# A fused macaron transformer block: two steps of VectorE's queue change places with the next item's cosines

## The reference, cut to what matters

```python
x = x + 0.5 * L0_ffn(layernorm(x))     # FFN stage, first time
x = x + L0_attn(layernorm(x))          # 16 heads, linear position bias
x = x + 0.5 * L0_ffn(layernorm(x))     # FFN stage, second time
x = x + 0.5 * L1_ffn(layernorm(x))     # mixture of 8 experts, top 1
x = x + L1_attn(layernorm(x))          # linear attention
x = x + 0.5 * L1_ffn(layernorm(x))
```

```python
h = shift_token(x); q, k, v = split(h @ wqkv)           # 8 heads of 64
q = l2norm(q) * qs; k = l2norm(k) * ks
q = q*cos*scale + rotate_half(q)*sin*scale               # k likewise with /scale
attn = softmax(mask(8 * q @ k.T)); x = x + (attn @ v) @ wo
h = layernorm(shift_token(x)) * g + b
a, g = split(h @ w1 + b1); x = x + (a * gelu(g)) @ w2 + b2
```

## Time and profile before

| | value |
|---|---|
| median of 3 runs | 2471.24 us (2462.63 to 2471.93) |
| profiled execution, own time | 2476.3 us |
| its span, first to last instruction | 2474.5 us |
| PE busy | 2133.3 us (86%) |
| DVE busy | 1762.1 us (71%) |
| ACT busy | 1464.2 us (59%) |
| POOL busy | 1056.6 us (43%) |

### The profile page before, as it was taken

One profiled execution on the slowest core, in us unless ns is written; L12 is line 12 of the kernel. 1 busy time (PEld: TensorE's weight loads), 2 busy tenths in 40 slices (PEclk: granted clock), 3 DMA queues, 4 the chain that ended last, 5 costly groups with the idle time before them and its releaser, 6 DMA issues. The chain is left out here.

```text
span 2474.5 us, 56322 instructions
## 1 busy us (share of the span) xinstructions
PE 2133.3 (86%) x23398; PEld 1572.0 (64%) x23398; DVE 1762.1 (71%) x2815; ACT 1464.2 (59%) x2389; POOL 1056.6 (43%) x800
## 2 busy tenths in 40 slices
PE   2799999999889868999878999999999897597968
PEld 1477676666666645555536767766666664495758
DVE  3678788788788637777727787887888884563556
ACT  0577676666666525666536776766667674363635
POOL 4656555454545210000036565555545450550245
PEclk8899999999999969999959999999999998698979
DMA  7000000089999990000000000000000003121022
GB/s 150 1 2 2 2 2 2 2 88 119 113 134 133 135 133 6 2 2 2 2 1 1 2 2 2 2 1 2 2 2 2 1 1 74 56 66 37 35 75 79
DMA packets 211376, 90.91 MB, mean 37 GB/s; under 512 B 79700, under 2 KB 206721, under 8 KB 210996
## 3 DMA queue, kind: packets, MB, share of 16 engines
q1 hardware_dynamic: 202596, 72.27, 23.7%
q0 software_dynamic: 6080, 11.76, 1.5%
q10 hardware_dynamic: 2448, 3.28, 0.6%
HBM read 24.31 MB, written 63.41 MB: 35 GB/s over the span
## 5 line engine op out<-in xcount | busy, mean ns | idle before, releaser
L490 POOL TENSOR_TENSOR work<-work,rot_tables 128x512 f32<-128x512 f32 x256 | 411.0, 1626 | 483.8 <-ACT work L594 483.8
L498 POOL TENSOR_TENSOR work<-work 128x1024 f32<-128x1024 f32 x128 | 304.5, 2379 | 53.0 <-DVE work L924 45.7
L1323 PE MATMUL psum<-qkv_w_hi,h_hi 128*128 128x512 f32 x384 | 189.6, 494 | 90.0 <-DVE small L948 87.7
L924 DVE TENSOR_TENSOR work<-work,rot_tables 128x1024 f32<-128x1024 f32 x128 | 211.0, 1648 | 19.2 <-ACT work L594 17.4
L941 DVE TENSOR_TENSOR work<-work,small 128x1024 f32<-128x1024 f32 x128 | 166.9, 1306 | 76.3 <-ACT small L608 72.1
L1081 DVE TENSOR_REDUCE small<-psum 128x4 f32<-128x1024 f32 x128 | 156.6, 1224 | 88.3 <-PE psum L1582 86.6
L1482 PE MATMUL psum<-centered,ffn_w 128*128 128x256 f32 x768 | 192.2, 402 | 3.0 <-DVE centered L985 2.9
L705 ACT ACTIVATE work<-psum 128x1024 f32<-128x1024 f32 x128 | 131.1, 1024 | 92.7 <-PE psum L1582 92.6
L1420 PE MATMUL psum<-work 64*128 64x128 f32 (+1 forms) x2048 | 179.3, 305 | 0.0
L632 ACT ACTIVATE squared<-centered 128x256 f32<-128x256 f32 x64 | 26.8, 419 | 244.9 <-DVE centered L981 244.9
L1482 PEld LDWEIGHTS psum<-centered,ffn_w 128*128 128x128 f32 x768 | 147.7, 199 | 30.7 <-DVE centered L985 4.5
(11 more groups left out here) (279 smaller groups left out, 5401.9 us busy)
## 6 DMA issues: line engine op xcount, KB each, us to landing
h_area<-mean_weights SPq DMA_DIRECT2D x24, 2048.0 KB, 27.7
tile_x<-h_area SPq DMA_DIRECT2D x39, 128.5 KB, 2.1
stage<-in_consts ACTq DMA_DIRECT2D x1, 2817.0 KB, 12.0
tile_x<-h_area SPq DMA_DIRECT2D x39, 64.5 KB, 1.8
work<-in_x SPq DMA_DIRECT2D x4, 512.0 KB, 27.7
expert_w<-in_ew SPq DMA_DIRECT2D x1, 2048.0 KB, 8.6
expert_w<-in_ew SPq DMA_DIRECT2D x8, 256.0 KB, 6.8
work<-y_tokens SPq DMA_DIRECT2D x4, 512.0 KB, 6.2
```

The lines of the kernel that those rows point to most:

```text
L490: last = pool.tensor_tensor(b[:, :, :, o_], a[:, :, :, i_], tab[:, l, 1, t, :, o_].unsqueeze(2).to_broadcast([P, 2, HEADS, 32]), ALU.mult)
L498: pool.tensor_tensor(rC[:, t, :], rC[:, t, :], rB[:, t, :], ALU.add).then_inc(f_sum, 1)
L924: dve.tensor_tensor(g(rC[:, t, :]), g(rA[:, t, :]), tab[:, l, 0, t, :, :].unsqueeze(2).to_broadcast([P, 2, HEADS, DH]), ALU.mult)\
L1323: pe.matmul(out, hi, w_hi, start=True, stop=False)
```

## The change

In DVE's queue the call `cosines(i, 0)` moves behind `s_max(i - 1, 0)` and `y_center(i - 2)`. No instruction is added, removed or altered, and no wait on a semaphore changes. In a step where all three parts exist, the order goes from cosines, first maximum (2 instructions), centering to first maximum, centering, cosines.

```diff
                     if old:
                         resid(i - 2)
-                    if new:
-                        cosines(i, 0)
                     if mid:
                         s_max(i - 1, 0)
                     if old:
                         y_center(i - 2)
+                    if new:
+                        cosines(i, 0)
                     if mid:
                         s_max(i - 1, 1)
                         s_max(i - 1, 2)
```

## The result

The changed kernel takes 2666.43 us (median of 4 runs, 2658.11 to 2676.37) against 2470.86 us before: ratio 1.079, 95% interval 1.075 to 1.083. The forecast was 2657 us, slower.

The account below looks back on a forecast made before the run. PE, busy 86%, was to be fed, with DVE's chain to `gated` setting late steps. Early steps 79.7, late 93.6 less 9.8, step 1s 2.4, together 166, plus clock 20: 186 on 2476.3 gives 2662, median 2657 us; range 2610 to 2695.

Parts of the forecast that it names:

- First maximum earlier: On DVE, L948 starts at R+0.14 instead of R+2.37 (R: end of `resid`); PE's wait of 1.96 or 0.87 us goes.
- Cosines unblocked: On DVE, first cosines start after POOL's two `sines` and take 1.23 us; saves 1.1 us in a late step.
- POOL's sum meets L963: L963 on DVE wants to start at R+4.90, amid POOL's `rotated` (R+3.17 to R+5.54), and is done at R+5.57.
- The second sines take turns with L964 and L985: L964 and L985 on DVE each wait through one POOL `sines` instruction; `gated` ends 2.60 us later in late steps.
- PE's clock: PE runs partly at 1.2 GHz after idle waits: nothing up to 1.0 us in each of 60 steps; 20 us taken.
- the wait for `gated`: PE's third group of scores_T waits for DVE's `gated`: 0.8 us of PE wait in the new step.
- the jam: DVE and POOL turns delay `gated`: 24 early steps x 3.32 = 79.7, 36 late x 2.60 = 93.6 less 9.8 us.
- The prediction's lock: DVE's and POOL's instructions on SBUF exclude one another as wholes; cosines take 2.32 us instead of 1.23 when blocked.

Follow-up runs that it names:

- v_proj twice: The changed kernel with every v_proj matmul issued twice, same values: 2637.85 us, ratio to before 1.065.
- `sines` held back a little less: The changed kernel with POOL's second sines waiting for `m_split`, which ends 0.3 us sooner than `y_normed`: 2561.98 us, ratio 1.037.

## Why the prediction was right

Point by point, on the late step shown above:

1. *First maximum earlier.* Right: it starts at R+0.15 (0.14 forecast), the centering ends at R+1.89 (1.76), 0.13 late since the two instructions don't overlap any more.
2. *Cosines unblocked.* Right: 1.22 us, and never blocked in any full step after.
3. *POOL's sum meets L963.* Right: 0.80 us.
4. *The second sines take turns with L964 and L985.* Right: medians over the 64 items are 0.80, 1.20 and 1.53 us for L963, L964 and L985, 1.37 for the clip. The three times that make the order held within 0.2 us: copy done at R+4.97 (about 4.9 forecast), sum over at R+5.55 (5.54), `m_split` wanting the port at R+4.79 (4.90). The experiments show it as a cause: holding the second `sines` back alone returns the whole loss.
5. *PE's clock.* Right in kind, low in size: I took 20 us. I expected the half-rate stretch in part of the steps; it came in 48 of 60. Three early steps became 2.4 us longer than those without one, more than the 1.0 us that I had as the upper bound. Where the stretch hits `up` it is only partly hidden behind the wait for `gated`: in the step shown PE reaches the third group of scores at 736.89, 0.85 us after `gated` has ended, so the wait for `gated` that I forecast is not there (0.82 us in v_proj twice).

As to the sum, 2.60 and 3.32 us per step were forecast. With the clock taken out (v_proj twice) they are 26.6 - 24.1 = 2.5 and 27.1 - 23.8 = 3.3. One reading under it was short: before, the clip collided in six late steps of 36, not five, which is 2 us.

The profiled executions let the terms be added up over steps 2 to 31. The 24 early steps take 571.4 us before, 650.1 with v_proj twice and 666.5 in the changed kernel; the 36 late ones 878.2, 956.2 and 977.7. So the jam without the clock is 78.7 + 78.0 = 156.7 us, where 79.7 + 83.8 were forecast, and the clock 37.9 us, where 20 were. One term was too large and the other too small: that 2657 came within 9 us of 2666 is in part luck. As v_proj twice changes PE's work too, the division is an estimate.

The prediction's lock was stated too widely. "DVE's and POOL's instructions on SBUF exclude one another as wholes" doesn't hold for the sums of squares L930, which read and write SBUF: in the late step of the earlier trace rows one of them runs beside POOL's `sines` and takes its usual time.

```profile
553.09 1.21 DVE L930 TENSOR_REDUCE small<-qk_squares 128x16 f32<-128x1024 f32 x1
```

All 128 of them take 1.21 to 1.22 us in the kernel before. The forecast doesn't suffer, as it took L930 at the time of its rows.

The prediction had set a page against the rows at L963. By the rows it waited, 0.62 us in the median, and so did the clip, 1.19 us, which has one input in SBUF as well. The Trainium skill's page SBUF — State Buffer (Who interferes with whom) lets a DVE instruction with one SBUF input pass unless it runs in a mode that uses both port pairs, and names `cast` and `tensor_scalar`, but on trn2 not `tensor_reduce`, among those that can enter such modes. L963 is a cast, the clip a `tensor_scalar`, L930 a `tensor_reduce`: the rows fit the page if the first two ran in such a mode, which no run here shows. Going with the rows was right.

## What to carry to other kernels

Before moving an instruction on VectorE, list which instructions of GpSimd read SBUF around the new place and which of VectorE's do so too, and lay the two queues against each other in time: an instruction of 0.2 us can take 1.2 us there, and where GpSimd has several in a row, each VectorE instruction pays one turn. A wait that looks like the bottleneck may keep two engines out of step in a useful way: removing PE's 1.96 us wait by moving one 0.4 us instruction too far cost 8%, and removing it with that instruction left in place won 1.2%. When a step works by such a phase, test the neighbouring orders; they differed by some 230 us here.

## What the runs showed of the hardware

- DVE and POOL took turns instruction by instruction. An instruction that was already waiting got in when the running one ended, also between two of the other engine's that stood back to back. How early it had to be there shows in the second cosines with the `sines` held back: in 60 steps they came 0.04 to 0.05 us before the end of POOL's first `sines` instruction (577.98 against 578.02) and got the turn; with the `sines` held back a little less they came 0.24 to 0.25 us after that end (609.43 against 609.18), in 60 steps too, and were blocked. The kernel before narrows it: in 33 late steps its first cosines came up to 0.02 us before that end (543.69 against 543.70 in the earlier trace rows) and were blocked all the same, for 1.1 us. So 0.04 us ahead was enough and 0.02 was not, by the recorded times.
- Not every instruction of DVE on SBUF took part: L963, L964, L985, L924, L941 and the clip waited for POOL, the `tensor_reduce` L930 never did (1.21 us throughout).
- Filling PE's waits with repeated matmuls made a kernel faster by 1.1% (2666.43 to 2637.85; the intervals of the ratios to before, 1.075 to 1.083 and 1.062 to 1.067, are apart), with the granted clock at 0.99 instead of 0.94 in the first stage. In the changed kernel PE's three waits of 0.85, 1.27 and 1.17 us come just before the slow stretch of a late step; with the second one filled, the stretch is gone in all of the 60 steps but one.
